# One audio tower layer on one Trainium2 core: new orders on all engines, mixing with 64 stationary columns, token weights through ScalarE's queue

## The chip, the cores and the metric

The kernel runs on one core of a Trainium2 chip. A core has TensorE (PE in the profile, its weight loads PEld), VectorE (DVE), ScalarE (ACT), GpSimd (POOL) and SyncE (SP). TensorE writes into PSUM, which has 8 banks of 512 fp32 values in each of 128 partitions; everything else lies in SBUF. The metric is the device time of one execution in microseconds (us), lower is better. The kernel before took 1020.71 us as the median of three runs (1018.73 to 1024.64).

## The reference, cut to what matters

```python
# x [128 batches, 64 features, 750 steps], padded to 752 = 94 windows of 8
scores  = einsum('bwkf,of->bwko', xp, w) + b          # token pooling
h       = sum(xp * softmax(scores, axis=2), axis=2)   # [128, 94, 64]
xn      = layernorm(h)
q, k    = xn @ Q[h], xn @ K[h]                        # 8 heads, rank 32
attn    = softmax(q @ k.T / sqrt(64))                 # [128, 8, 94, 94]
h       = h + sum_h (attn @ xn) @ VO[h]
h       = h + ffn(layernorm(h))
# ffn: 4 heads x 4 experts of causal attention with width 16, a gated sum of the
# experts, layernorm, two 16x16 layers with a mask, layernorm, and a gate over the heads
```

All arithmetic is fp32. "Mixing" in the title is `attn @ xn`.

## The kernel before, in words

The 128 batches go through in 32 quads of four. Partitions hold 4 batches x 32 tokens, and the free dimension holds the three token blocks j = 0, 1, 2. Nothing is scheduled by the hardware or a compiler: each engine has its own function `quad(g)` that lists its steps in an order written out by hand, and calls it for g = 0 to 42 or 43. A step works on quad g - d, where d is the step's distance: so one call holds steps of up to 13 different quads, and the distances make a software pipeline. Steps wait on semaphores (`wait_ge`). PSUM banks are given to steps by number, so a step also waits until the last reader of its bank is done.

The steps on TensorE, with their lines, in the order in which a quad meets them: `tok_score` (L598, token scores for two quads at a time), `tok_turn` (L612), `turn` (L588, transposes of x into three banks), `pool_x` (L606, the pooled h), `turn_x` (L650), `project` (L657), `score` (L665, one call for each block j), `mix` (L676), `give_outT` (L686), `give_out` (L697), `front_turn` (L703), `front_pair` (L710), `front_sv` (L716, L719), `score3_a` (L743) and `score3_b` (L759), the expert scores, `turn_p3` (L766), `mix3` (L776), `turn_c` (L785), `turn_rest` (L803), `layer1` (L807), `layer2` (L811), `turn_fo` (L790) and `head_logits` (L797).

What lies around the places that the change touches:

- `mix` (L676) multiplies, for each block `ub`, the weights `pT` by `xn`. A stationary operand is a 32x32 piece of `xn`; the loops over 2 parities, 2 column halves `c` and 4 batches use all 16 pieces of the array. The accumulation runs over the three `ub`. An fp32 matmul is two LDWEIGHTS and two MATMUL instructions here. `mix` waits for ScalarE's `front_kp` (L1101) to empty its banks.
- `exp_s` (L1074) is the softmax exponential on ScalarE, 8 ACTIVATEs per block j; `exp_s(0)` follows `front_kp` directly, and `layer2` on TensorE waits for it, because both use bank 6. `copy_cT` (L1079) empties the mixed result and follows `exp_s(0)` on ScalarE.
- `soft` (L1368, L1370) is VectorE's maximum and subtraction for the expert scores; `soft(2)` follows `score3_a` and frees the banks for `mix3`.
- GpSimd applies the softmax denominators (`norm_p`, L462), the two steps of the layer norms with a power (`norm_power` L495, `ln_power` L450, `power3` L467) and the gates. VectorE's `turn_p(0)` (L1349) waits for `norm_p(0)`.
- Before the loops GpSimd clears constants and then loads the token weights and bias by three DMAs of its own (L414 to L416). TensorE waits for these three and for the x of quad 0 before the first `tok_score`.
- SyncE loads x for quads 0 to 5 first, the attention weights (q, k, vo) between them, then some 60 small, strided loads of the feed-forward weights (L346), and only then enters its own loop of x loads and stores. `make_g` (L620, once) needs the attention weights, `split_w` (L1300, L1301, VectorE, once) and after it `make_w` (L629, TensorE, once) need all of the feed-forward weights.

On TensorE before, the calls begin as follows: g = 0 is `tok_score(0)`; g = 1 is `make_g`, `tok_turn`, two of the `turn`s of quad 0; g = 2 is the third `turn`, `pool_x(0)`, `tok_score(2)`, two `turn`s of quad 1; g = 3 is the third, `turn_x(0)`, `pool_x(1)`, `project(0)`, the three `score(0)`, `tok_turn`, `make_w`, two `turn`s of quad 2; g = 4 is the third, `turn_x(1)`, `pool_x(2)`, `project(1)`, `score(1)`, `mix(0)`, `score(1, j=2)`, `give_outT(0)`, `tok_score(4)`, `give_out(0)`, and two `turn`s of quad 3.

Of the kernel before, what the change touches and what calls it, by code (L numbers as in the profile page):

```python
# [15 lines left out]
TP = 96  # L16
# [26 lines left out]
def audio_tower(nc, x, tok_w, tok_b, attn_q, attn_k, attn_vo, hl_w, hl_b, wq, wk, wv, gate_w, gate_b,  # L43
                ln_g, ln_b, fc1_w, fc1_b, fc2_w, fc2_b, fnorm_g, fnorm_b, fgate_w, out):
    with ExitStack() as ctx:
# [24 lines left out]
        zeroed = sem("zeroed")  # L70
        zeroed2 = sem("zeroed2")
# [255 lines left out]
        def _(sp):  # L327
# [57 lines left out]
            def quad(g):  # L385
                if exists(g + 6, NQUAD):
                    sp.wait_ge(x_turned, 3 * g + 3)
                    load(g + 6)
                if exists(g - 12, TAIL):
                    sp.wait_ge(ho_made, 3 * g - 33)  # L390
                    store(g - 12, (g - 12) % 2)
                if TAIL <= g - 12 < NQUAD:
                    sp.wait_ge(ho_made_late, 3 * g - 120)
                    store(g - 12, (g - 12) % 2)

            for g in range(44):
                quad(g)
# [5 lines left out]
        def _(pool):  # L403
            pool.memset(ident_w[:, :], 0.0).then_inc(zeroed, 1)
# [4 lines left out]
            pool.memset(tw[:, :], 0.0).then_inc(zeroed, 1)  # L409
            pool.memset(wp[:, :, :, :], 0.0).then_inc(zeroed, 1)  # L410
            pool.memset(xs[:, :, NTIME:128 * NCH], 0.0).then_inc(zeroed, 1)
            pool.wait_ge(zeroed, 8)
# [111 lines left out]
            def quad(g):  # L524
                if exists(g - 11, TAIL):
                    finish(g - 11)
                if exists(g, NQUAD):
                    if g < 4:
                        pool.wait_ge(tok_ready, (g) // 2 + 1)
                    weigh(g)  # L530
# [3 lines left out]
                if exists(g - 2, NQUAD):  # L534
                    pool.wait_ge(at_summed, 3 * g - 3)
                    norm_p(1, at_normed)
                if exists(g - 2, NQUAD):
                    norm_p(2, at_normed)
                if exists(g - 6, NQUAD):
                    pool.wait_ge(y_eps, g - 5)  # L540
                    norm_power(g - 6, 0, y_rstd)
# [3 lines left out]
                if exists(g - 6, TAIL):  # L545
                    pool.wait_ge(y_rstd, 2 * g - 10)
                    scale(0, y_mul)
# [3 lines left out]
                if exists(g - 1, NQUAD):  # L551
                    pool.wait_ge(at_summed, 3 * g - 2)
                    norm_p(0, at_normed)
                if exists(g - 7, TAIL):
                    pool.wait_ge(t_made, g - 6)
                    residual()
                if exists(g - 8, NQUAD):
                    if g - 8 >= 28:
                        pool.wait_ge(z_eps, g - 7)
                    norm_power(g - 8, 1, z_rstd)  # L560
                if exists(g - 5, NQUAD):
                    pool.wait_ge(g_inv, 2 * g - 8)
                    gate_weight(g - 5)
                if exists(g - 6, TAIL):
                    norm_affine(g - 6, 0, fx_made, "j h", fx[:, :, 0:96].rearrange("p h (j c) -> p j h c", c=32))
                if exists(g - 5, NQUAD):
                    pool.wait_ge(g_weight, 2 * g - 8)
                    gate_mul((g - 5) % 2)
# [3 lines left out]
                if exists(g - 2, NQUAD):  # L572
                    pool.wait_ge(ln3_var, 2 * g - 2)
                    power3(g - 2)
                if exists(g - 8, TAIL):
                    scale(1, z_mul)
# [5 lines left out]
        def _(pe):  # L582
# [62 lines left out]
            pe.wait_ge(zeroed, 8)  # L645
# [168 lines left out]
            def quad(g):  # L814
                if exists(g - 7, NQUAD):
                    if g - 7 >= 29:
                        pe.wait_ge(t_made, g - 9)
                    if g - 7 < 29:
                        pe.wait_ge(at_exped, 3 * g - 9)
                    turn_p3(4, 6, p_turned)  # L820
                if exists(g - 7, NQUAD):
                    if g - 7 < 27:
                        pe.wait_ge(x_copied, 2 * g - 3)
                    if 27 <= g - 7 < 30:
                        pe.wait_ge(at_added, g - 4)
                    turn_p3(3, 0, p_turned)
                if exists(g - 12, NQUAD):
                    pe.wait_ge(fo_copied, g - 11)
                    head_logits(7)
                if exists(g - 2, NQUAD):  # L830
                    if g - 2 >= 5:
                        pe.wait_ge(p_exped, 6 * g - 37)
                    if 2 <= g - 2 < 5:
                        pe.wait_ge(at_exped, 3 * g - 9)
                    turn(g - 2, 2, 6, x_turned)
                if g - 1 == 0:
                    make_g(3)
                if g - 6 == 0:
                    front_resid(7)
                if exists(g - 9, NQUAD):  # L840
                    if g - 9 < 30:
                        pe.wait_ge(p_exped, 6 * g - 36)
                    if g - 9 >= 29:
                        pe.wait_ge(fx_made_late, 2 * g - 74)
                    if g - 9 < 29:
                        pe.wait_ge(fx_made, 2 * g - 16)
                    turn_rest(fx[:, :, :], 0, r1_fxt)
                if exists(g - 7, NQUAD):
                    if g - 7 < 27:
                        pe.wait_ge(x_copied, 2 * g - 2)  # L850
                    if g - 7 < 31:
                        pe.wait_ge(s_shifted2, 2 * g - 10)
                    mix3(g - 7, 1)
                if exists(g - 3, NQUAD):
                    if g - 3 < 4:
                        pe.wait_ge(x_copied, 2 * g - 3)
                    if g - 3 >= 6:
                        pe.wait_ge(r1_fxc, g - 8)
# [738 lines left out]
```

## Time and profile before

| | |
|---|---|
| median of three runs | 1020.71 us |
| profiled execution, device time | 1028.39 us |
| profiled execution, span of the trace | 1026.7 us |
| instructions | 53,493 |
| busy: PE, PEld | 875.7 us (85%), 602.5 us (59%) |
| busy: DVE, ACT, POOL | 754.3, 741.7, 693.8 us (73%, 72%, 68%) |
| chain that ended last | PE 62%, ACT 17%, DVE 11%, issue 4%, SPq 4%, POOL 2% |
| granted TensorE clock, mean | 0.963 |

The profiled execution is 7.7 us slower than the median of the runs. A share of the chain is the part of the span for which the work followed back from the end stood on that engine. "Issue" is time in which an engine waited for nothing that the profile shows. TensorE's busy time is the union of overlapping matmuls, whose ends are modelled.

### The profile page before, as it was taken

To read this page: it belongs to the slowest core of one execution; us is meant where nothing else is said; L and a number is where in the kernel's file an instruction comes from. 1 tells how busy PE (TensorE), PEld (TensorE's weight loads), DVE (VectorE), ACT (ScalarE), POOL (GpSimd) and SP (SyncE) were. 2 spreads that over 40 slices of the span, in tenths; PEclk is the share of its full clock that TensorE was granted. 3 is DMA by queue.
4 is the path that set the end of the run, shared out by engine and by line. 5 is a ranking of instruction groups with operands and counts; after the bars stand their busy time and mean duration, and the time that the engine had idled before them with its cause. 6 is when DMAs were issued, how large, how long until landed. Compare 5 with 4: busy or idle time off the path is not lost.

```text
span 1026.7 us, 53493 instructions
## 1 busy us (share of the span) xinstructions
PE 875.7 (85%) x23616; PEld 602.5 (59%) x23616; DVE 754.3 (73%) x1786; ACT 741.7 (72%) x2631; POOL 693.8 (68%) x1087
## 2 busy tenths in 40 slices
PE   4488988998898989899999999998998998887853
PEld 3365655665665656566676666665676665555531
DVE  2346677777777788778888788877888888776765
ACT  1567777887777888777887788887887787774521
POOL 3343345666678677677788777776777877766684
PEclk9789999999999999999999999999999999999965
DMA  6211111001111110011111111001000000000000
GB/s 191 66 62 33 33 34 33 27 11 33 33 33 37 38 36 24 18 38 37 38 38 38 37 37 38 15 27 41 7 9 7 7 7 7 4 8 6 11 8 21
DMA packets 34504, 31.47 MB, mean 31 GB/s; under 512 B 26080, under 2 KB 26080, under 8 KB 34272
## 3 DMA queue, kind: packets, MB, share of 16 engines
q1 hardware_dynamic: 33926, 28.00, 9.4%
q8 instruction: 185, 3.03, 1.2%
q14 instruction: 47, 0.39, 0.1%
q10 hardware_dynamic: 250, 0.05, 0.0%
q0 software_dynamic: 96, 0.00, 0.0%
HBM read 24.95 MB, written 3.08 MB: 27 GB/s over the span
## 4 chain that ended last, share of the span: by engine, by line
PE 62%; ACT 17%; DVE 11%; issue 4%; SPq 4%; POOL 2%; DMA 0%; POOLq 0%
PE psum L676 8%; ACT pu L1074 8%; PE psum L776 7%; PE psum L785 6%; PE psum L766 6%; PE psum L657 4%; PE psum L759 4%; PE psum L710 4%; DVE pu L1370 4%; DVE mx L1368 4%; ACT cT L1079 3%; PE psum L665 3%; SPq L346 2%; PE psum L606 2%; ACT kp L1101 2%
## 5 line engine op out<-in xcount | busy, mean ns | idle before, releaser
L1074 ACT ACTIVATE pu<-psum,mx 128x94 f32<-128x94 f32 x768 | 250.7, 386 | 4.0 <-DVE mx L1343 4.0
L1074 ACT ACTIVATION_READ_ACCUMULATOR pu<-psum,mx 128x1 f32 x768 | 194.7, 254 | 0.0
L462 POOL TENSOR_TENSOR pu<-pu,pr 128x752 f32<-128x752 f32 x96 | 137.4, 1445 | 23.9 <-DVE pr L1346 23.8
L1368 DVE TENSOR_REDUCE mx<-psum 128x16 f32<-128x1536 f32 (+2 forms) x96 | 117.2, 1221 | 48.3 <-PE psum L759 30.7
L495 POOL TENSOR_TENSOR st<-st,neg_half 128x12 f32<-128x12 f32 x64 | 146.2, 2285 | 5.0
L448 POOL TENSOR_TENSOR ln_ve<-ln_mv,eps_c 128x3 f32<-128x3 f32 x32 | 6.2, 193 | 178.8 <-DVE ln_mv L1338 178.8
L1343 DVE TENSOR_REDUCE mx<-psum 128x8 f32<-128x752 f32 x96 | 89.0, 927 | 46.1 <-PE psum L665 46.1
L1370 DVE TENSOR_TENSOR pu<-psum,mx 128x1536 f32<-128x1536 f32 (+2 forms) x96 | 117.6, 1225 | 3.3
L665 PE MATMUL psum<-kp,xT 64*32 64x376 f32 x1536 | 103.1, 486 | 17.4 <-DVE ft L1440 11.6
L1112 ACT ACTIVATE pT<-psum 128x512 f32<-128x512 f32 x192 | 104.5, 595 | 14.4 <-PE psum L766 12.5
L766 PE MATMUL psum<-ident_w,pu 128*128 128x128 f32 x768 | 102.1, 277 | 1.0 <-ACT pu L1074 0.6
L676 PE MATMUL psum<-pT,xn 32*32 32x384 f32 x3072 | 88.5, 491 | 9.6 <-ACT kp L1101 8.6
L1349 DVE STREAM_TRANSPOSE pT<-pu 128x768 f32<-128x768 f32 x96 | 89.7, 958 | 4.5 <-POOL pu L462 4.5
L766 PEld LDWEIGHTS psum<-ident_w,pu 128*128 128x128 f32 x768 | 87.6, 142 | 3.9 <-ACT pu L1074 1.2
L1375 DVE SCALAR_TENSOR_TENSOR ct<-sxT,psum 128x512 f32<-128x512 f32 x96 | 60.3, 684 | 32.3 <-PE psum L776 32.3
L785 PE MATMUL psum<-gx,ct 128*32 128x84 f32 x3072 | 74.1, 242 | 8.2 <-issue 6.7
L776 PE MATMUL psum<-pT,vv 32*32 32x384 f32 (+2 forms) x3072 | 70.9, 403 | 10.9 <-DVE pu L1370 9.7
L676 PEld LDWEIGHTS psum<-pT,xn 32*32 32x32 f32 x3072 | 45.2, 103 | 52.4 <-ACT kp L1101 30.7
L785 PEld LDWEIGHTS psum<-gx,ct 128*32 128x32 f32 x3072 | 61.9, 139 | 21.8 <-issue 19.5
L1115 ACT ACTIVATE oc<-psum 128x336 f32<-128x336 f32 x96 | 43.3, 452 | 38.8 <-PE psum L785 32.1
L1064 ACT ACTIVATE xT<-psum 128x384 f32<-128x384 f32 x32 | 15.7, 491 | 72.5 <-PE psum L650 72.4
L710 PE MATMUL psum<-x3T,aq 64*32 64x384 f32 x1024 | 65.8, 483 | 1.2 <-ACT hx L1121 1.2
(185 smaller groups left out, 2123.8 us busy)
## 6 DMA issues: line engine op xcount, KB each, us to landing
xs<-in_x SPq DMA_DIRECT2D x64, 375.0 KB, 3.8
out_h<-ho SPq DMA_DIRECT2D x126, 16.0 KB, 1.8
out_h<-ho SPq DMA_DIRECT2D x126, 7.5 KB, 1.8
gx<-in_L_ffn_gate_w SPq DMA_DIRECT2D x16, 0.2 KB
fc<-in_L_ffn_fc_w SPq DMA_DIRECT2D x12, 1.0 KB
fc<-in_L_ffn_fc_b SPq DMA_DIRECT2D x12, 0.1 KB
vo_w<-in_L_attn_VO SPq DMA_DIRECT2D x2, 64.0 KB, 8.7
q_w<-in_L_attn_Q SPq DMA_DIRECT2D x1, 64.0 KB, 7.8
```

Of the source, the lines that this page charges most:

```text
L462: pool.tensor_tensor(p, p, bcast(pr[:, j, :, :].rearrange("p a b -> p (a b)"), 2, NTOK), ALU.mult).then_inc(done, 1)
L495: pool.tensor_tensor(st[:, k, 3, :], st[:, k, 2, :], neg_half[:, 0:NJ * NH], ALU.pow).then_inc(rstd, 1)
L665: mm = pe.matmul(psum[TB * b:TB * b + TB, bank + par, 0:HP * NTOK], xT[rows, n % 2, b, TB * j:TB * j + TB], kp[rows, n % 2, b, :, 0:NTOK], ...
L676: mm = pe.matmul(psum[q:q + 32, bank + b, 0:HP * TP].rearrange("p (h j t) -> p h j t", h=HP, j=NT), xn[rows, n % 4, ub, 0, 32 * c:32 * c + ...
L710: mm = pe.matmul(psum[32 * n:32 * n + 32, bank + half, 0:NJ * 128], aq[rows, e + half, n, :], x3T[rows, :, :].rearrange("p b t -> p (b t)" ...
L766: mm = pe.transpose(psum[:, bank, 128 * e:128 * e + 128], pu3[j][:, e, k, :, :].rearrange("p b u -> p (b u)"), ident)
L776: mm = pe.matmul(psum[QB * n:QB * n + QB, bank + b, 128 * k:3 * 128].rearrange("p (j t e) -> p j e t", e=NE, t=QB), vv[rows, n3 % 2, k, n, ...
L785: mm = pe.matmul(psum[rows, bank, GC * e:GC * e + GC], ct3[:, j, rows, e], gx[:, e, :], start=True, stop=True)
L1074: ins = act.activation(pu[:, j, par, hp, 0:NTOK], psum[:, bank + par, NTOK * hp:NTOK * hp + NTOK], ACT.Exp, bias=mx[:, j, par, hp:hp + 1], ...
L1112: act.activation(pT3[:, SLOT3[P3[f]], :, :].rearrange("p e c -> p (e c)"), psum[:, bank, :], ACT.Exp).then_inc(done, 1)
L1368: dve.tensor_reduce(mx3[:, j, :, :], S3(j, bank), AX.X, ALU.max).then_inc(shifted, 1)
L1370: dve.tensor_tensor(pu3[j][:, :, :, :, :].rearrange("p e k b u -> p b e k u"), S3(j, bank).rearrange("p b e (k u) -> p b e k u", u=QB), bc ...
```

## The change

1. `mix`: the stationary operand is now 64 columns wide (`xn[rows, ..., :]`), so a matmul fills a 32x64 piece of the array; the loop over `c` is gone, and the order is `ub`, batch, parity. 24 matmuls for each quad in place of 48.
2. The token weights and the bias are loaded by ScalarE's queue, the bias without any wait, the weights after a semaphore of their own (`tw_zeroed`) that GpSimd's first instruction sets.
3. The order inside `quad(g)` is new on all four computing engines, with other distances, other waits and other PSUM banks. On TensorE the call now begins where `score(j=2)` stood: most of the new distances are the old ones less one, because the loop's start was moved by most of a call. Apart from that start, `turn_x` comes before `mix3`, `turn_rest` after it, `turn_p3(4)` between two `turn`s, `layer1` before `front_turn`.
4. `make_g` moves from g = 1 to g = 2, behind `turn(1)`; `make_w` from g = 3 to g = 4, behind `give_out(0)`.
5. SyncE stores quad g - 13 instead of g - 12 and runs 45 calls in place of 44; TensorE runs 43 calls in place of 44.

TensorE's first calls are now: g = 0 `tok_score(0)`; g = 1 `tok_turn`, the three `turn`s of quad 0, `pool_x(0)`; g = 2 `tok_score(2)`, three `turn`s, `make_g`, `turn_x(0)`, `pool_x(1)`, `project(0)`, `score(0)` for j = 0, 1; g = 3 `score(0, j=2)`, `tok_turn`, three `turn`s of quad 2, `turn_x(1)`, `pool_x(2)`, `project(1)`, `score(1)`, `mix(0)`; g = 4 `score(1, j=2)`, `give_outT(0)`, `tok_score(4)`, `give_out(0)`, `make_w`, `turn`s of quad 3.

```diff
@@ SyncE, quad(g)
-                if exists(g - 12, TAIL):
-                    sp.wait_ge(ho_made, 3 * g - 33)
-                    store(g - 12, (g - 12) % 2)
+                if exists(g - 13, TAIL):
+                    sp.wait_ge(ho_made, 3 * g - 36)
+                    store(g - 13, (g - 13) % 2)
@@ GpSimd, start
+            pool.memset(tw[:, :], 0.0).then_inc(tw_zeroed, 1)
             pool.memset(ident_w[:, :], 0.0).then_inc(zeroed, 1)
...
-            pool.dma_start(tw[0:NFEAT, 26:27], tok_w.rearrange("o f -> f o")).then_inc(tok_loaded, 16)
-            pool.dma_start(tw[NFEAT:128, 32:33], tok_w.rearrange("o f -> f o")).then_inc(tok_loaded, 16)
-            pool.dma_start(tokb[:, :], tok_b.partition_broadcast(128)).then_inc(tok_loaded, 16)
@@ GpSimd, quad(g): the new order, waits left out
+   norm_power(g-9, 1), residual (g-8), norm_p(0) (g-2), scale(0) (g-7), gate_weight(g-6), scale(1) (g-9),
+   gate_mul (g-6), norm_affine(g-7, 0), norm_affine(g-9, 1), norm_p(1) (g-2), weigh(g), power3(g-3),
+   norm_p(2) (g-2), finish(g-11), norm_power(g-6, 0), ln_power(g), gate_scale (g-5), ln_apply(g)
@@ GpSimd, quad(g): the order before
-   finish(g-11), weigh(g), norm_affine(g-9, 1), norm_p(1), norm_p(2) (g-2), norm_power(g-6, 0), ln_power(g),
-   scale(0) (g-6), gate_scale (g-5), norm_p(0) (g-1), residual (g-7), norm_power(g-8, 1), gate_weight(g-5),
-   norm_affine(g-6, 0), gate_mul (g-5), ln_apply(g), power3(g-2), scale(1) (g-8)
@@ TensorE, mix
                 for ub in range(NT):
-                    for par in range(2):
-                        for c in range(2):
-                            for b in range(4):
-                                rows = slice(TB * b, TB * b + TB)
-                                q = 64 * par + 32 * c
-                                mm = pe.matmul(psum[q:q + 32, bank + b, 0:HP * TP].rearrange("p (h j t) -> p h j t", h=HP, j=NT),
-                                               xn[rows, n % 4, ub, 0, 32 * c:32 * c + 32],
-                                               pT[rows, :, par, :, ub, :].rearrange("p j h t -> p h j t"), start=(ub == 0), stop=(ub == NT - 1))
+                    for b in range(4):
+                        rows = slice(TB * b, TB * b + TB)
+                        for par in range(2):
+                            mm = pe.matmul(psum[64 * par:64 * par + 64, bank + b, 0:HP * TP].rearrange("p (h j t) -> p h j t", h=HP, j=NT),
+                                           xn[rows, n % 4, ub, 0, :], pT[rows, :, par, :, ub, :].rearrange("p j h t -> p h j t"),
+                                           start=(ub == 0), stop=(ub == NT - 1))
@@ TensorE, quad(g), steady part: the new order, waits left out, banks in brackets
+   score j=2 (g-3) [6], give_outT(g-4) [2], tok_score(g) [0], tok_turn [3], give_out(g-4) [1], score3_a(g-5) [2],
+   turn 0 (g-1) [1], turn_p3 4 (g-6) [0], turn 1 (g-1) [6], turn_fo(g-11) [7], turn_p3 3 (g-6) [1], turn 2 (g-1) [0],
+   turn_x(g-2) [7], head_logits(g-11) [6], mix3(g-6) [1], turn_rest (g-8) [5], turn_p3 0, 1 (g-5) [6, 7],
+   turn_c 0 (g-6) [5], score3_b(g-5) [0], turn_c 2, 1 (g-6) [7, 5], pool_x(g-1) [4], turn_p3 2 (g-5) [6],
+   layer1 (g-8) [7], front_turn (g-4) [5], turn_p3 5 (g-5) [4], project(g-2) [6, 2], front_pair 0 (g-4) [4],
+   front_sv [0], score j=0 (g-2) [6], front_pair 2 [2], score j=1 [4], mix(g-3) [0], layer2 (g-8) [6]
@@ ScalarE, start
+            act.dma_start(tokb[:, :], tok_b.partition_broadcast(128)).then_inc(tok_loaded, 16)
+            act.wait_ge(tw_zeroed, 1)
+            act.dma_start(tw[0:NFEAT, 26:27], tok_w.rearrange("o f -> f o")).then_inc(tok_loaded, 16)
+            act.dma_start(tw[NFEAT:128, 32:33], tok_w.rearrange("o f -> f o")).then_inc(tok_loaded, 16)
@@ VectorE, quad(g), steady part: the new order, waits left out
+   head_sum(g-12), sums 0 (g-3), mask_second (g-9), least 2 (g-3), turn_p 0 (g-3), sums 1 (g-3), gate_sum(g-7),
+   soft_tok(g), add_out(g-4), soft(g-5, j=2), head_shift(g-11), stats3(g-4), copy_x 2 (g-1), sums 2 (g-3),
+   guard 0, 1, 2 (g-6), mix_experts(g-7), centre(g-9), soft j=0 (g-5), variance(0) (g-7), soft j=1, sums_inv (g-6),
+   ln_stats(g-1), turn_p 1, mask_hidden (g-8), turn_p 2, variance(1) (g-9), least 0 (g-2), gate_shift(g-6), least 1
...
```

## Rows read from the trace of the kernel before

**Rows 1.** Stretches of the span: length, then each engine's busy us (instructions), clock, DMA.
```profile
0.00:81.50 81.50, 50.23 (x923) 35.86 (x925) 28.66 (x102) 36.96 (x140) 28.78 (x62) 0.85 0.36 101
512.63:568.66 56.03, 52.28 (x1465) 36.51 (x1465) 45.84 (x110) 45.94 (x165) 43.72 (x68) 1.00 0.12 35
934.80:1026.70 91.90, 54.48 (x1247) 36.03 (x1247) 57.80 (x155) 28.75 (x74) 59.19 (x88) 0.75 0.05 11
```

**Rows 2.** Chain that ended last, two calls: start us, us, what.
```profile
511.77 0.82 ACT kp L1101
...
512.63 2.77 PE psum L676 x94
515.40 0.63 PE psum L811 x4
...
525.45 2.11 PE psum L776 x73
```

**Rows 3.** The same chain over the whole span, starts of mixing: first, clean pair, last.
```profile
133.94 2.78 PE psum L676 x94
...
540.25 2.78 PE psum L676 x94
...
880.92 2.78 PE psum L676 x94
```

**Rows 4.** A stretch inside mixing: busy PE (count), PEld (count), clock, DMA.
```profile
513.45:513.80 0.35, 0.35 (x33) 0.31 (x31) 1.00 0.20 47
```

**Rows 5.** TensorE's timeline, projection; then its group by shape (busy us, mean ns).
```profile
507.23 1.52 PE L657 MATMUL psum<-xT,g_w 64*32 64x384 f32 x32
...
L657 PE MATMUL psum<-xT,g_w 64*32 64x384 f32 x1024 | 50.1, 497 | 1.6 <-DVE pu L1370 0.9 <-ACT pT L1112 0.7
```

**Rows 6.** ScalarE's timeline around mixing.
```profile
514.68 0.38 ACT L1074 ACTIVATE pu<-psum,mx 128x94 f32<-128x94 f32 x1
515.43 1.51 ACT L1079 ACTIVATE cT<-psum 128x768 f32<-128x768 f32 x2 [0.28 <-PE psum L676]
```

**Rows 7.** Waits over the whole span: total us, times, longest us.
```profile
PEld psum L811 <- ACT pu L1074: 16.3, 26, 0.6
PEld psum L606 <- issue: 15.3, 14, 1.6
```

**Rows 8.** Timeline of the start, POOL's queue and TensorE.
```profile
4.35 0.57 POOL L416 DMA_DIRECT2D tokb<-in_L_tok_b  x1
...
11.96 2.79 PE L598 MATMUL psum<-xs,tw 128*32 128x128 f32 x48 [11.96 <-DMA tokb<-in_L_tok_b]
...
16.80 1.59 PE L620 MATMUL psum<-q_w,k_w 32*64 32x64 f32 x16 [2.05 <-DMA vo_w<-in_L_attn_VO]
16.81 0.29 DVE L1287 TENSOR_TENSOR tok_e<-tok_e,tok_r 128x128 f32<-128x128 f32 x1
18.32 0.47 PE L612 MATMUL psum<-ident_w,tok_e 128*128 128x128 f32 x1
```

**Rows 9.** Loads of x for quad 0 (issued 0.8 to 2.2): us to landing.
```profile
DMA to landing us min/median/max: 3.4/4.5/5.7
```

**Rows 10.** Timeline of TensorE from 39 us to 66 us.
```profile
39.02 0.48 PE L612 MATMUL psum<-ident_w,tok_e 128*128 128x128 f32 x1 [0.40 <-DVE tok_e L1287]
...
64.43 0.54 PE L697 MATMUL psum<-ident_w,oT 64*32 64x64 f32 x24
```

**Rows 11.** Chain of the start: the last feed-forward weight, then `make_w`.
```profile
41.12 4.85 DMA bet<-in_L_ffn_fnorm_b
...
46.94 1.03 PE psum L629 x32
```

**Rows 12.** DMA queue of TensorE's instructions: packets, MB, share of 16 engines.
```profile
q8 instruction: 185, 3.03, 1.2%
```

**Rows 13.** GpSimd and VectorE around the first softmax block.
```profile
515.50 1.44 POOL L462 TENSOR_TENSOR pu<-pu,pr 128x752 f32<-128x752 f32 x1
518.34 0.96 DVE L1349 STREAM_TRANSPOSE pT<-pu 128x768 f32<-128x768 f32 x1
```

More of the change, by code:

```diff
@@ L827, in quad @@
[L827 to L853, printed above, removed]
@@ L966, in quad @@
                     pe.wait_ge(at_cT, 2 * g - 6)
[L967 removed]
+                    give_outT(2)
+                if exists(g, NQUAD) and (g) % 2 == 0:
+                    tok_score(g, 0)
                 if exists(g - 1, NQUAD) and (g - 1) % 2 == 0:
[L969 to L972 removed]
+                    if g - 1 < 7:
+                        pe.wait_ge(tok_normed, (g - 1) // 2 + 1)
+                    tok_turn(3)
                 if exists(g - 4, NQUAD):
                     pe.wait_ge(at_oT, g - 3)
[L975 to L976 removed]
+                    give_out(1)
+                if g - 4 == 0:
                     pe.wait_ge(w_split, 1)
[L978 removed]
+                    make_w(2)
                 if exists(g - 5, NQUAD):
@@ new lines, in quad @@
+                if exists(g - 1, NQUAD):
+                    if g - 1 >= 5:
+                        pe.wait_ge(p_exped, 6 * g - 31)
+                    if g - 1 == 1:
+                        pe.wait_ge(tok_shifted, (g + 1) // 2 + 1)
+                    if g - 1 == 3:
+                        pe.wait_ge(tok_shifted, (g + 1) // 2 + 1)
+                    turn(g - 1, 2, 0, x_turned)
+                if exists(g - 2, NQUAD):
+                    if g - 2 >= 9:
+                        pe.wait_ge(fo_copied, g - 10)
+                    if g - 2 < 2:
+                        pe.wait_ge(ln_done, 2 * g - 2)
+                    turn_x(g - 2, 7)
@@ L1027, in _ @@
+                if exists(g - 8, NQUAD):
+                    if g - 8 < 26:
+                        pe.wait_ge(at_exped, 3 * g - 5)
+                    pe.wait_ge(h_masked, g - 7)
+                    layer2(6)
+            for g in range(0, 43):
                 quad(g)
@@ L1136, in quad @@
             def quad(g):
+                if exists(g - 4, NQUAD):
+                    act.wait_ge(at_mixed, g - 3)
+                    copy_cT(1, 0, at_cT)
+                if exists(g - 4, NQUAD):
+                    copy_cT(0, 0, at_cT)
+                if exists(g - 3, NQUAD):
+                    act.wait_ge(at_maxed, 3 * g - 7)
+                    exp_s(1, 4, at_exped)
+                if exists(g - 4, NQUAD):
+                    act.wait_ge(at_outT, g - 3)
+                    copy_oT(2)
@@ new lines, in quad @@
+                if exists(g - 1, NQUAD) and (g - 1) % 2 == 0:
+                    act.wait_ge(tok_turned, (g - 1) // 2 + 1)
+                    copy_tok(g - 1, 3)
+                if exists(g - 7, NQUAD):
+                    if g - 7 >= 28:
+                        act.wait_ge(g_shifted, 3 * g - 18)
+                    gate_exp()
+                if exists(g - 3, NQUAD):
+                    act.wait_ge(at_maxed, 3 * g - 6)
+                    exp_s(2, 6, at_exped)
+                if g - 4 == 0:
+                    act.wait_ge(w_made, 1)
+                    copy_m(2)
@@ new lines, in quad @@
+                if exists(g - 5, NQUAD):
+                    soft(g - 5, 1, 0, s_shifted1)
+                if exists(g - 6, NQUAD):
+                    dve.wait_ge(c_copied, 3 * g - 15)
+                    sums_inv((g - 6) % 2)
+                if exists(g - 1, NQUAD):
+                    dve.wait_ge(h_pooled, g)
+                    ln_stats(g - 1)
+                if exists(g - 3, NQUAD):
+                    turn_p(1, at_pturned)
+                if exists(g - 8, NQUAD):
+                    dve.wait_ge(r1_hx, g - 7)
+                    mask_hidden()
```

667 lines of the change are left out of this document (323 added, 344 removed).

## The prediction

> **What bounds the kernel now.** I read the stretches first, then the chain that ended last, the waits on it, and the timelines around single steps. The span has three parts. The fill (0 to 81.5 us) has TensorE busy for only 50.2 us, the steady part 52.3 of every 56.0, and the tail from 934.8 us 54.5 of 91.9 [rows 1]. In the steady part TensorE is the bound at the full clock: its mixing is on the chain in every call, and starts 747.0 us apart from the first to the last of 26 calls, 28.73 us a call [rows 3]. The pair 512.63 to 540.25 takes 27.6 us [rows 2, 3], so an average call loses 1.1 us that a clean one doesn't. Most of it is "issue" idleness in the dense runs of small matmuls: 14 waits before L606 alone, up to 1.6 us each, 15.3 us in all [rows 7].
>
> **Change 1, mixing.** 96 MATMULs take 2.77 us on the chain [rows 2]. They go through the array as 3 rounds (`ub`) of 2 passes. What a pass costs where loads keep up is shown by the projection: 4 passes of 8 pieces with the same 384 columns take 1.52 us [rows 5]; less one matmul's 0.50 us at the end [rows 5] that is 3 steps of 0.34. Six passes at that price are 5 x 0.34 + 0.50 = 2.2 us. Mixing takes 0.57 us longer, and a row shows how: within its second round 31 weight loads are issued in 0.35 us [rows 4], so they had not been pulled ahead of the matmuls, as a round of 16 pieces is 64 instructions. The new rounds have 8 pieces and 32 instructions, like the projection's. I take 2.2 us: a gain of 0.57 us for each quad. Bounds: 0, if what costs is the columns and not the loads; and a loss, if 32x64 pieces with four row groups don't run side by side. No row has such a piece, so the worst end is by the projection's passes at double number: 12 steps, 11 x 0.34 + 0.5 = 4.2 us, a loss of 1.5 us for each quad.
> The Trainium skill (TensorE: Matmul & The Clock Gate, Part 2: What happens when you issue a matmul) gives TensorE a window of 64 instructions in which it pulls weight loads ahead. The row agrees with that reading; the sum doesn't need it.
>
> How much of 0.57 us reaches the end? `front_kp` on ScalarE (0.82 us from 511.77) releases mixing and then starts `exp_s(0)` at once [rows 2]. Its last ACTIVATE starts at 514.68 and, with its accumulator read, is over at about 515.15 [rows 6]; `layer2`, next on TensorE, waits for exactly that in 26 calls [rows 7]. Mixing ends at 515.40 [rows 2]. So in the calls where TensorE is the chain, `layer2` gains about 0.15 us, not 0.57. Where ScalarE is the chain (the other parity, in which `give_out` waits for it), `copy_cT` had been idle 0.28 us for mixing [rows 6] and gains that. 16 x 0.15 + 16 x 0.28 = 7 us; **I take -6**, ends 0 and -18 (0.57 x 32, if nothing hides it).
>
> **Change 3, the orders.** Listed by quad and not by call, nearly every distance is unchanged: the call starts elsewhere. What remains on TensorE is a swap around `mix3` (`turn_x` before, `turn_rest` behind) and new banks. In one parity `mix3` waits for VectorE's `soft(2)` (it starts at 525.45 [rows 2], after `score3_a` plus two passes of VectorE), in the other for copies on ScalarE whose sum is the same; neither list is shorter. I cost it at 0. Cover: the 0.05 us that the swap adds before `mix3` lies in that wait. On GpSimd `norm_p(0)` now stands behind `norm_power(1)` and `residual`, which waits for VectorE's `mask_second`. Before, it ran 515.50 to 516.9 and `turn_p(0)` took its result only at 518.34 [rows 13]. I place it about 1.5 us later, which ends at 518.4, just when VectorE arrives, and VectorE then waits anyway for `exp_s(1)`. GpSimd is busy 43.7 of 56.0 us [rows 1], so it can hold the order. Bounds: nothing to 2 us a call, see the fourth rival. The tail has the same steps at the same distances: 0, with 4 us either way.
>
> **Change 2 and 4, the start.** (a) TensorE starts at 11.96, held by the bias, which GpSimd issued at 4.35 as the third of its loads [rows 8]. x of quad 0 needs at most 5.7 us after an issue at 2.2 at the latest, so it is there at 7.9 [rows 9]. ScalarE's queue has nothing before and can issue near 0.8 to 2.5 us. If its landing takes the bias's 7.4 us (4.35 to 11.75), TensorE starts at 9 to 10, if as long as x, at 8. Gain 2 to 4, I take 3.5. The Trainium skill (DMA: Bandwidth & Descriptors, SWDGE vs HWDGE vs iDMA) says that the queue of ScalarE makes descriptors in hardware and sets up faster than GpSimd's; by that it would be the 4. (b) `make_g` waits for the attention weights and holds `tok_turn`, which starts at 18.32 though its input is ready at 17.1 [rows 8]: -1.2. It comes back later at its own 1.6 us [rows 8]: +1.6. (c) After `tok_turn` at 39.02 to 39.5 TensorE has nothing but `make_w`, which waits for the last feed-forward weight (landing at 46.0) and starts at 46.94 [rows 10, 11]. The new order puts the steps from `turn(2)` to `give_out(0)` before it, which now run from 47.97 to 64.97, 17.0 us [rows 10, 11]. New: 39.5 - 3.1 + 17.0 = 53.4, past 46.9, so `make_w` no longer waits, and the 7.4 us of idleness are filled. Sum: 3.5 + 1.2 - 1.6 + 7.4 = 10.5 us; **I take -11** with the better chance of a warm clock. Bounds: -5 (the freed time is eaten by the latency of softmax chains, that before ran during the wait) to -15.
>
> **Instruction supply.** TensorE's instructions come in 185 packets of 3.03 MB [rows 12], 256 instructions of 64 bytes each, and the losses before L606 are at every 256th. A boundary costs only if it falls in the dense run from `turn_c` to `pool_x`. Counting positions through both lists (47,232 instructions before, 3,072 fewer now), 17 calls were hit before and about 13 would be now, at about 1.8 us. **I take -5**, for the count slips easily; ends +5 and -15.
>
> **Change 5.** A later store is cost at 0: the buffers' next writer is 2 quads away, and at the end the last store still follows the last result.
>
> **Sum.** -6 - 11 - 5 = -22 us. Against the profiled execution's 1028.4 that is 1006.4; it stood 7.7 above the median of the runs, and for the median I subtract the same 22 us: 1020.7 - 22 = **999 us**.
>
> **The rivals.**
> 1. *Mixing is bound by columns and the supply doesn't improve.* Only the start remains: -11, 1010 us. For it: a pass of 384 columns costs the same in both shapes; against: rows 4. The Trainium skill (TensorEngine Tiling (Array Packing), Overview) measures the gain by the number of pieces: 3 rounds before, 3 rounds now, nothing gained. Its time is this one; the trace bears it out only in part, since 16 pieces cost more a pass than 8. Chance 0.22.
> 2. *The cover of mixing is thinner than I read*, so 0.57 us goes through in most calls, and supply gains 10: -11 - 16 - 10 = -37, 984 us. Against: `layer2`'s wait [rows 7]. Chance 0.15.
> 3. *Slower: the 32x64 pieces don't run side by side.* Mixing becomes 4.2 us, past `exp_s(0)`, so all of +1.45 reaches the end in each of 32 quads: +46 - 11 - 5, 1051 us. It decides as soon as mixing lasts over 2.9 us. Against: `score` and projection run 8 pieces in two row groups. Chance 0.05.
> 4. *GpSimd's order is late.* If `norm_p(0)` ends over 1 us after 518.4, `turn_p(0)` holds VectorE, `soft(2)` and `mix3` behind it, at about 0.7 us a call: +22 - 22 = 0, 1021 us. Against: GpSimd's idleness of 6 us a call. Chance 0.08.
>
> **How the numbers follow.** My forecast has 0.50. The 8 in 10 range takes rival 1, most of 2 and the bounds of the start: 982 to 1015. The likeliest case alone spans 992 to 1006. A measurement here tells 0.5% (5 us) from no change: faster than 1015.6 is my case, rivals 1 and 2 nearly whole, 0.85; within 5 us 0.07; slower 0.08 (rival 3 and the bad half of 4).
>
> **What would show it.** In the new profile: mixing at 2.2 us on the chain, but the next `layer2` waiting for `exp_s(0)` for longer than 0.6 us; the first `tok_score` at 8 to 10 us; `make_w` without a wait at about 53 us; `mix3` preceded by the same waits; fewer "issue" losses at L606, L759, L785; a clean call near 27.4. I am wrong if mixing doesn't shrink, if `turn_p(0)` waits for GpSimd in most calls, or if the early scores come no sooner than before.

## The result, and the profile after

The changed kernel takes 996.7 us (median of 4 runs, 996.1 to 1000.1), the kernel before, beside it on the same chip, 1021.6 us (4 runs, 1018.7 to 1024.6). The ratio is 0.9757, with a 95% interval of 0.9722 to 0.9792: 25 us less, where the forecast said 22. The profiled executions are further apart, 1028.4 against 996.1 us, and so are their spans, 1026.7 and 994.4 us: the one of before stood above its median, the one of after at it.

The stretches of the span, cut as in [rows 1] at the second start of mixing, over two calls, and from the last start of mixing (length, then each engine's busy us and instructions, clock, DMA):

```profile
0.00:70.70 70.70, 46.49 (x870) 32.84 (x870) 29.55 (x103) 36.93 (x140) 30.03 (x64) 0.86 0.38 116
487.99:545.10 57.11, 51.33 (x1369) 35.76 (x1369) 46.22 (x109) 45.75 (x166) 45.06 (x69) 1.00 0.11 34
906.10:994.40 88.30, 50.88 (x1199) 34.72 (x1199) 57.10 (x152) 28.00 (x74) 58.71 (x87) 0.79 0.05 12
```

The fill is 10.8 us shorter than in [rows 1] and the tail 3.6. The two calls are 1.1 us longer than the pair of [rows 1]; each call of this pair has a halt of the instruction stream, and the first of that one had none. A pair says little here; 26 calls say more, below.

The groups of mixing and projection by shape (busy us, mean ns), and then the queue of TensorE's instructions (packets, MB), which answer to [rows 2, 5] and [rows 12]:

```profile
L675 PE MATMUL psum<-pT,xn 32*64 32x384 f32 x1536 | 70.2, 490 | 9.5 <-ACT kp L1110 9.5
...
L658 PE MATMUL psum<-xT,g_w 64*32 64x384 f32 x1024 | 50.1, 494 | 0.1
```
```profile
q8 instruction: 173, 2.83, 1.1%
```

Mixing keeps TensorE busy for 70.2 / 32 = 2.19 us a quad: the forecast's 2.2. A stretch of the second round, as [rows 4] (busy PE, PEld, DVE, ACT, POOL, clock, DMA):

```profile
488.90:489.25 0.35, 0.35 (x23) 0.21 (x12) 0.35 (x2) 0.35 (x4) 0.35 (x1) 1.00 0.00 0
```

12 weight loads issue in 0.35 us, where it was 31. Half of that drop is the halved number of loads. The rest is their pace: in the trace groups of 8 matmuls now follow each other by 0.34 us, nearly all with 8 loads, while before a round's 31 or 32 loads fell into 0.35 us and the round's last matmuls went on without any. The Trainium skill (TensorE: Matmul & The Clock Gate, Part 2: What happens when you issue a matmul) has loads pulled ahead within 64 instructions; with rounds of 32 instructions this row agrees. No run changed the number of instructions in a round alone, so that the window is what cost the 0.57 us is not shown.

The chain that ended last, around one start of mixing, and the wait of `layer2` on `exp_s(0)` over the whole span, which answer to [rows 2, 7]:

```profile
487.18 0.81 ACT kp L1110
487.99 2.58 ACT pu L1083 x16
490.57 0.04 issue
490.61 0.70 PE psum L810 x4
491.31 0.02 issue
491.33 0.37 DVE ft L1451
```
```profile
PEld psum L810 <- ACT pu L1083: 27.1, 26, 1.0
```

Mixing has left the chain. The step from the copy of kp goes through ScalarE's exponentials (L1083) to `layer2` (L810); that wait grew from 16.3 to 27.1 us over 26 calls, from 0.63 to 1.04 us a call. So 0.41 of the 0.57 us turn into waiting there: it is the cover that the prediction named.

GpSimd and VectorE around the first softmax block, which answer to [rows 13]:

```profile
492.32 1.45 POOL L460 TENSOR_TENSOR pu<-pu,pr 128x752 f32<-128x752 f32 x1
493.80 0.98 DVE L1360 STREAM_TRANSPOSE pT<-pu 128x768 f32<-128x768 f32 x1
```

Counted from the start of mixing, `norm_p(0)` runs 4.33 us later, where it ran 2.87 later before: moved by 1.5 us as worked out. VectorE takes its result 5.81 us after that start, against 5.71 before. Its own work lasts until then, and in none of the 96 times does it wait for GpSimd (4 times before, 4.5 us): nothing is lost.

The chain of the start:

```profile
2.19 6.37 DMA xs<-in_x
8.57 0.14 issue
8.70 2.79 PE psum L599 x48
...
13.87 0.33 PE psum L613
...
53.45 0.03 DVE whl L1311
53.48 0.32 DVE whl L1312
53.80 1.33 DVE whl L1311
55.12 0.32 DVE whl L1312
...
57.04 1.53 PE psum L589 x12
```

The first scoring of tokens (L599) now waits for x itself and starts at 8.70, not 11.96; `tok_turn` starts at 13.87, not 18.32. `make_w` is held by VectorE's `split_w` (L1311, L1312) rather than by a DMA. The first full `turn` behind it starts at 57.04; it was at 65.79.

Last, what the prediction called instruction supply. A stretch of the chain in the dense part of a call, in the changed kernel's first profile, and the same call in a second profile of the same kernel (e12):

```profile
506.33 1.33 PE psum L784 x64
507.66 0.44 PE psum L607 x31
508.10 0.57 issue
508.67 0.44 PE psum L607 x17
509.11 0.59 PE psum L765 x4
```
```profile
504.67 1.33 PE psum L784 x64
506.00 0.44 PE psum L607 x31
506.44 1.12 issue
507.56 0.44 PE psum L607 x17
508.00 0.59 PE psum L765 x4
```

In both, `pool_x` stops behind the same matmul, its 31st, with nothing to wait for: once for 0.57 us, once for 1.12. I call this a halt, and count it from the traces' list of TensorE's instructions: an instruction that starts over 0.15 us after the one before it, and whose place in the list is 193 plus a multiple of 256. (A true wait that falls there is counted too.) In the kernel before the halts of the 26 calls come to 30.7 us, in the changed one to 20.6. By the waits over the whole span the idleness without a releaser fell too: of the weight loads from 15.3 to 10.1 us at `pool_x` [rows 7], from 6.7 to 3.0 at `score3_b` and from 19.5 to 16.0 at `turn_c`, but it rose from 9.1 to 16.0 at `mix3`. The prediction had the waits before `mix3` unchanged, and they aren't: its MATMULs wait for VectorE's `soft` for 21.4 us in 31 calls, before for 9.7 us in 18.

### The profile page after: what moved, and what is told of

Its sections match the earlier page's. It is cut to its first block, busy times and chain, and to the rows that moved or that the text cites. A ratio compares the mean times of both kernels' runs of the same rounds, so it can differ in the third digit from the quotient of the medians.

```text
span 994.4 us, 50395 instructions
## 1 busy us (share of the span) xinstructions
PE 847.6 (85%) x22080; PEld 588.5 (59%) x22080; DVE 756.6 (76%) x1786; ACT 737.6 (74%) x2631; POOL 694.4 (70%) x1084
## 4 chain that ended last, share of the span: by engine, by line
PE 57%; ACT 21%; DVE 16%; issue 3%; POOL 2%; DMA 1%; POOLq 0%; SPq 0%; DVEq 0%
ACT pu L1083 13%; PE psum L775 7%; DVE pu L1381 6%; DVE mx L1379 6%; PE psum L784 6%; PE psum L765 6%; PE psum L658 5%; PE psum L709 4%; PE psum L758 4%; PE psum L742 3%; PE psum L666 3%; ACT cT L1088 3%; PE psum L607 3%; ACT kp L1110 3%; PE psum L599 2%
## 5 line engine op out<-in xcount | busy, mean ns | idle before, releaser
L1083 ACT ACTIVATE pu<-psum,mx 128x94 f32<-128x94 f32 x768 | 254.4, 425 | 4.0 <-DVE mx L1354 4.0
L1083 ACT ACTIVATION_READ_ACCUMULATOR pu<-psum,mx 128x1 f32 x768 | 215.5, 293 | 0.0
L1121 ACT ACTIVATE pT<-psum 128x512 f32<-128x512 f32 x192 | 115.1, 616 | 20.6 <-PE psum L765 19.9
L666 PE MATMUL psum<-kp,xT 64*32 64x376 f32 x1536 | 105.6, 485 | 19.4 <-DVE ft L1451 11.6
L765 PE MATMUL psum<-ident_w,pu 128*128 128x128 f32 x768 | 115.0, 280 | 1.5 <-DVE pu L1381 1.3
L775 PE MATMUL psum<-pT,vv 32*32 32x384 f32 (+2 forms) x3072 | 69.7, 396 | 21.6 <-DVE pu L1381 21.4
L1127 ACT ACTIVATE fxT<-psum 128x256 f32<-128x256 f32 x32 | 12.3, 384 | 95.0 <-PE psum L802 95.0
L675 PE MATMUL psum<-pT,xn 32*64 32x384 f32 x1536 | 70.2, 490 | 9.5 <-ACT kp L1110 9.5
L775 PEld LDWEIGHTS psum<-pT,vv 32*32 32x32 f32 x3072 | 45.0, 104 | 41.1 <-ACT pT L1121 16.2
L589 PE MATMUL psum<-ident_w,xs 128*128 128x128 f32 x384 | 61.6, 288 | 8.3 <-ACT pu L1083 6.8
L510 POOL TENSOR_TENSOR ft<-ft,fx 128x192 f32<-128x192 f32 x29 | 17.2, 594 | 68.7 <-DVE ft L1451 68.7
```

The source lines that it names most:

```text
L666: mm = pe.matmul(psum[TB * b:TB * b + TB, bank + par, 0:HP * NTOK], xT[rows, n % 2, b, TB * j:TB * j + TB], kp[rows, n % 2, b, :, 0:NTOK], ...
L765: mm = pe.transpose(psum[:, bank, 128 * e:128 * e + 128], pu3[j][:, e, k, :, :].rearrange("p b u -> p (b u)"), ident)
L775: mm = pe.matmul(psum[QB * n:QB * n + QB, bank + b, 128 * k:3 * 128].rearrange("p (j t e) -> p j e t", e=NE, t=QB), vv[rows, n3 % 2, k, n, ...
L1083: ins = act.activation(pu[:, j, par, hp, 0:NTOK], psum[:, bank + par, NTOK * hp:NTOK * hp + NTOK], ACT.Exp, bias=mx[:, j, par, hp:hp + 1], ...
L1121: act.activation(pT3[:, SLOT3[P3[f]], :, :].rearrange("p e c -> p (e c)"), psum[:, bank, :], ACT.Exp).then_inc(done, 1)
```

## The experiments

Eleven other kernels ran, and the changed one again (e12), each beside the kernel before (medians there 1022 to 1024 us). Ratios are to that kernel.

**e1 to e4: one part alone, or all but one.** The edit of e1 (e2 is its reverse, in the changed kernel):

```diff
-for par in range(2): for c in range(2): for b in range(4):
-    pe.matmul(psum[q:q + 32, ...], xn[rows, n % 4, ub, 0, 32 * c:32 * c + 32], pT[...])
+for b in range(4): for par in range(2):
+    pe.matmul(psum[64 * par:64 * par + 64, ...], xn[rows, n % 4, ub, 0, :], pT[...])
```

> The kernel before with the 64-column mixing alone. Theory A (the prediction's): a call's mixing falls from 2.77 to about 2.2 us, but the softmax's exponentials on ScalarE (2.58 us after the copy of kp) take its place as the end of that stretch, so only about 0.2 us of a call's 0.57 reach the end: some 6 us less than the kernel before, ratio about 0.994. Rival B: the whole 0.57 us of 32 calls reaches the end: 18 us less, ratio 0.982. Rival C: mixing was never on the path that sets the end: within 2 us. The change also takes 64 TensorE instructions out of each call, so it moves the places at which TensorE's stream halts without a wait; by a table from the trace before, their sum stays at 27 us, so no more than 3 us either way is expected of that.

> The changed kernel with the old 32-column mixing put back, all else as changed. Theory A: some 6 us more than the changed kernel (996.7), about 1003. Rival B (the whole 0.57 us of 32 calls): about 1015. Rival C: about 997. Theory S (the halts of TensorE's stream at every 256th instruction depend on which instruction stands there): the added instructions move the halts of the dense stretches, whose sum by a table from the two traces rises from 20 to some 30 us, so about 1010 with theory A.

Measured: e1 0.9948 (0.9923 to 0.9973), 5 us less. (It takes 96 instructions out of a call, not the 64 expected: 24 matmuls at 4.) e2 0.9943 (0.9913 to 0.9972), 1017.0 us: 20 us more than the changed kernel. So mixing seemed to be worth 5 us in one place and 20 in the other. Shares of the chain by line, e1 and then e2:

```profile
ACT pu L1072 16%; PE psum L774 7%; PE psum L783 7%; PE psum L764 5%; PE psum L657 4%; PE psum L708 4%; PE psum L757 4%; DVE pu L1368 4%; DVE mx L1366 4%; PE psum L665 3%; ACT cT L1077 3%; ACT kp L1099 3%; SPq L346 3%; PE psum L606 2%; PE psum L684 2%
```
```profile
PE psum L677 9%; PE psum L777 7%; PE psum L786 7%; PE psum L767 6%; DVE pu L1383 6%; DVE mx L1381 6%; ACT pu L1085 5%; PE psum L658 5%; PE psum L711 4%; PE psum L760 4%; PE psum L666 3%; ACT cT L1090 3%; PE psum L744 3%; PE psum L607 3%; ACT kp L1112 3%
```

In e1 mixing (L674) is gone from the list and the exponentials (L1072) have 16%, twice the 8% of L1074 before; in e2 mixing (L677) leads with 9%. The wait of `layer2` for the exponentials goes with mixing alone: 26.9 us in e1, 16.3 in e2, as 27.1 and 16.3 in the kernels of after and before. So the cover is shown both ways:

```profile
PEld psum L809 <- ACT pu L1072: 26.9, 26, 1.0
```
```profile
PEld psum L812 <- ACT pu L1085: 16.3, 26, 0.6
```

e2's time is that of rival B (1015) and not theory A's 1003; why it is not rival B's mechanism the table below tells.

The edits of the start, e3 the loads alone, e4 both:

```diff
-pool.dma_start(tokb[:, :], ...)          # and the two loads of tw
+act.dma_start(tokb[:, :], ...)           # first on ScalarE's queue
...
-if g - 3 == 0: make_w(3); copy_m(3)
+if g - 4 == 0: make_w(3); copy_m(3)      # and split_w later in that call
```

> The kernel before with the three token loads on ScalarE's queue alone. Theory A: the first scoring of tokens (L598) starts when x has landed, about 8.7 us, and not at 11.96, and the gain is carried to the end: 3.3 us less, about 1018. Rival D: the start is bound again further on, by the filter and the weights (make_w), so nothing reaches the end: within 1 us of the kernel before.

> The kernel before with both edits of the start: the token loads on ScalarE's queue, and the making of the second filter's weights (make_w, with the split and the copy that follow it) one call later. Theory A: the 7.4 us that TensorE waited for make_w are filled and 3.3 us come from the loads: 9 to 11 us less, about 1011. Rival D: the first front stages are bound elsewhere (VectorE's softmax of the tokens and split), so under 4 us: about 1018.

Measured: e3 1.0007 (0.9980 to 1.0034), no gain; e4 0.9893 (0.9866 to 0.9920), 10.9 us less. TensorE's timeline in e3:

```profile
9.67 2.79 PE L596 MATMUL psum<-xs,tw 128*32 128x128 f32 x48 [9.67 <-DMA xs<-in_x]
15.12 1.60 PE L618 MATMUL psum<-q_w,k_w 32*64 32x64 f32 x16 [2.66 <-DMA vo_w<-in_L_attn_VO]
16.65 0.47 PE L610 MATMUL psum<-ident_w,tok_e 128*128 128x128 f32 x1
```

The scoring starts 2.3 us sooner, but `make_g` (L618) still waits for the attention weights, which land at 15, and holds `tok_turn` (L610) to 16.65, 1.7 us sooner than in [rows 8]. Later the wait for `make_w` takes the rest: mixing of quad 0 starts at 56.7, before at 57.0.

**e5 and e8: do the parts add?** e5 is e1 and e4 in one; e8 is e4 with the loads left on GpSimd's queue.

> The kernel before with the 64-column mixing and both edits of the start. Singly these gave 5.1 us (mixing, e1) and 10.8 us (start, e4). Theory A (the terms add, and the new orders give nothing of their own): about 1007, and then the 10 us between this and the changed kernel (996.7) are neither mixing nor start, so the orders or the places of TensorE's halts. Rival M (mixing is worth more where the start is short): about 997, and the orders are worth nothing.

> The kernel before with the making of the second filter's weights one call later and the token loads left on GpSimd's queue. Theory A (the prediction's: the two edits are worth 7.4 and 3.5 us): 3 us more than the kernel with both edits (e4, 10.8 us under before), so about 7.5 us under before. Rival D: the loads are worth nothing with or without it (alone they gave nothing, e3): the same 10.8 us under before.

Measured: e5 0.9841 (0.9810 to 0.9872), 16.3 us less; e1 and e4 add up to 5.3 + 10.9 = 16.2. e8 0.9909 (0.9881 to 0.9937), 9.3 us less. Singly the parts add, and 8 us are left between e5 and the changed kernel (0.9764 in e12). e8 and e4 are 1.6 us apart, within their intervals; that the loads then count is not shown by it.

**Where each kernel's time is.** From the traces, in us: start of mixing of quad 3 (the fill), the 26 calls from there to that of quad 29, the halts within them, the mean of those calls with under 0.25 us of them, and from there to the end. The calls were also fitted, for each kernel by itself, to a straight line over their halts:

```
kernel                     fill   26 calls  halts  clean call  rest   us of call per us of halt
before                     133.9   747.0    30.7    27.48     145.7   1.03
e1 mixing                  134.5   730.9    22.6    27.26     144.3   1.03
e3 loads                   133.7   742.2    27.1    27.47     149.2   1.00
e8 make_w later            128.0   742.3    28.3    27.48     146.5   1.02
e4 e3 and e8               126.8   736.4    22.6    27.49     145.6   0.93
e5 e1 and e4               124.0   737.0    29.8    27.27     144.8   1.07
e2 after, mixing as before 130.4   743.3    30.7    none      148.8   1.04
after                      125.8   727.0    20.6    27.15     141.5   1.04
e12 after again            124.1   726.4    20.4    27.09     142.8   1.09
```

A microsecond of halt makes its call a microsecond longer, in every kernel. That is a fit over 26 calls, not an intervention, but nine kernels agree. And a clean call takes 27.47 to 27.49 us with the old mixing and old orders, 27.26 or 27.27 with the new mixing in them, and 27.09 to 27.15 in the changed kernel. With no halt at all the last two are 27.21 or 27.26 and 27.15 or 27.22, from 5 to 7 calls each: what the new orders give a clean call is not clear of that.

The list of TensorE's instructions doesn't fix the sum of the halts. From quad 2 on, the kernel before, e3, e4 and e8 have the same list, to within one instruction, and their halts are 30.7, 27.1, 22.6 and 28.3 us. The profiled executions of the four lie +5.4, +3.1, -1.7 and +3.6 us from their kernels' medians: about as much as their halts differ. So an execution's halts are part of its noise, and the halts of two single profiles compare kernels only roughly.

From before to after the spans differ by 32.3 us: fill 8.1, halts 30.7 - 20.6 = 10.1, the rest of the calls (747.0 - 30.7) - (727.0 - 20.6) = 9.9, tail 4.2. e2 against after, 28 us in the spans: fill 4.6, halts 10.1, rest of the calls 6.2, tail 7.3. So e2's 20 us in the medians are not mixing's own time: putting it back also adds 96 instructions a call, and so moves every later halt. How much of the 20 the halts are is not shown, as e2's profiled execution is 7 us slower than its median.

**e6, e7, e9, e10, e11: moving the halts.** In the traces up to then, a call had no halt between mix3 and pool_x if the first such place lay about 124 to 178 instructions behind the start of mix3. These kernels add instructions that compute nothing new, to bring it there or away from it.

```diff
+def pad(k):                                  # e6, e7: waits already met
+    for _ in range(k): pe.wait_ge(tw_zeroed, 1)
...
+for i in range(fills.get(n, 0)):             # e9, e10, e11: ahead of mix
+    pe.matmul(psum[64 * par:64 * par + 32, bank + b, 0:1], xn[..., 0:32], pT[..., 0:1], start=True, stop=True)
```

> The changed kernel with waits that are already met put into TensorE's stream: 112 ahead of its first instruction, and 62 spread over four places in every second call (654 in all), so that the first 256th instruction after the start of each call's layer-2 mixing (mix3) falls on its 124th to 182nd instruction in 20 of the 26 calls from the fifth on. Theory S: in all traces so far the stretch from mix3 to pool_x takes 7.4 to 7.5 us and has no halt where that instruction lies between 124 and 205, and 8.2 to 10 us elsewhere; most of the changed kernel's 20.6 us of halts go, less what the added waits cost (650 of 20 to 50 ns, most while TensorE waits anyway): 8 to 17 us less, 980 to 989. Rival W: the halts come from something in time (a transfer, another engine), not from the place in the stream: no gain, and up to 10 us more for the waits, 997 to 1007.

> The same 654 met waits at the same places, with 72 more between the first scoring of tokens and the first transposition, where TensorE waits about 2 us anyway: all later instructions are the same as in the run before it, 72 places further on, so that the 256th instruction falls on the 61st or the 110th of mix3. Theory S: a halt of about 1.2 us in nearly every call, so about 30 us over the run against about 5 us of the kernel with 72 fewer: 20 to 30 us slower than that one, 1005 to 1015. Rival W: the same time as that one within 2 us.

> The changed kernel with tiny matmuls (32 columns of weights, one moving column, into PSUM cells that mix writes over) ahead of mix: 56 instructions before mix(0) and mix(1) each, and 62 before every second later mix, so that by the trace of the changed kernel the 256th instruction of TensorE's stream falls on the 127th or the 176th instruction from the start of mix3 in the calls of n = 4 to 25. Theory S: those 22 calls have no halt between mix3 and pool_x (0 to 0.3 us each, the run of 7.4 us), where the changed kernel had 17 us; less about 0.4 us for each of 10 groups: 10 to 15 us under the changed kernel in the same session. Rival W (the halts follow time or transfers): the same halts at other calls, no gain.

> The same with 96 more of the tiny instructions before mix(0) and mix(1), all later ones the same: the 256th instruction falls on the 31st or the 80th of mix3. Theory S: about 1.4 us in each of the 22 calls, 30 us of halts, and 20 to 30 us more than the kernel with 96 fewer. Rival W: within 2 us of it.

> The kernel before with the 64-column mixing and both edits of the start (e5, whose profile has 29.5 us of halts), and tiny matmuls ahead of mix, placed so that the 256th instruction falls on the 148th or the 199th from the start of mix3. Theory S: nearly all of the 25 us of halts of those calls go, 15 to 22 us less than e5, 986 to 994, and the new orders by themselves are worth what then separates it from the changed kernel placed in the same way. Rival W: no gain on e5, 1008.

> The changed kernel again, beside the three others on the same chip: 996 to 1001, with halts of 18 to 24 us at the same calls as in its first profile if they hang on the place in the stream alone (theory S), at other calls if not.

Measured, with the halts of the 26 calls counted as in the table: e6 0.9802 (1005.2 us) with 25.4 us, e7 0.9826 (1006.9) with 24.8; e9 0.9888 (1010.2) with 26.5, e10 0.9880 (1009.2) with 25.8; e11 0.9871 (1008.4) with 22.4, e5 having 29.8; e12 0.9764 (0.9731 to 0.9798) with 20.4, the first profile 20.6. Not one gained. The reason is in the traces: the placings were not the ones planned. Two of the added waits make one instruction in most places (654 waits gave 374), and one of the tiny f32 matmuls makes four (369 gave 1,476 instructions), not the two that I had counted. So "good" and "bad" both passed through all places in turn, their halts are alike, and their times with them. As a test of what a good placing is worth, these five failed, and it stays untried.

They do show three things. First, e12 halts at the same calls as the first profile; per call, the two correlate with 0.91. The kernel before and e3 do with 0.94, but e4 and e8 only with 0.65, though both have one list: two calls have 1.8 and 2.2 us of halts in e8 and none in e4. Second, where instructions were put in, the halts moved as the place says. With the new orders (after and e2, e6, e7, e9, e10, e12; the 24 calls from quad 2 on each) by the distance of the first place from mix3:

```
distance   124-177  178-212  213-240  241-255  0-60   61-123
calls         34       18       23       14     37      42
mean halt   0.02     0.40     0.63     1.66    1.46    1.28  us
```

None of the 34 calls in the first column has a halt over 0.25 us; 77 of the 79 in the last two have. With the old orders the free stretch is 124 to 212, 51 of 53 calls. Rival W in its plain form, that halts follow time and not the place, falls. Third, an added wait costs, and not only by itself. In e6 `layer2` (L821) starts 0.24 us after the exponentials, and 0.04 in the changed kernel. The added waits there, 106 ns each and not the 20 to 50 expected, were over 0.6 us earlier; but `layer2`'s own two waits now stand in the trace as instructions of their own.

```profile
496.79 2.57 ACT pu L1098 x16
499.36 0.24 issue
499.60 0.67 PE psum L821 x4
```

**What a halt waits for.** The traces also list the packets of the queue that moves TensorE's instructions, and there are as many as places at every 256th instruction. They are paired here in order, the first packet with the second place, in all 14 traces between 130 and 880 us. The packet of a place starts 0.85 us (median) after the place before it was passed and takes 0.99 us. The instruction at the place never starts sooner than 1.17 us after the end of its packet, and 387 of the 424 halts end 1.17 to 1.60 us after it; where there is no halt, the median is 3.4 us. Where TensorE went through the 256 instructions ahead of a place in under 3.0 us, halt left out, 250 of 268 places halted; over 4.0 us, 89 of 1466, true waits among them. So the halt ends when the next instructions have arrived, and it appears where TensorE uses them up faster than they come. Here rival W is half right: a transfer ends the halt, but the place in the stream sets when the transfer starts and how soon its instructions are needed. This is read from traces; no run changed the transfers.

## Why the prediction came out right

Its sum was -22, measured is -25 (medians); the terms, in the profiles that it was worked out from:

- *Mixing 2.77 to 2.2 us, of which -6 reach the end.* The duration is 2.19. Alone it gives -5.3 us (-7.9 to -2.8, moved halts among it), and 0.22 us a clean call. The cover was read rightly: `exp_s(0)` ends what mixing ended before. Rival 1 (columns bind, nothing gained) falls with e1; so does the forecast's reading of the Trainium skill (TensorEngine Tiling (Array Packing), Overview), which gives speedups by the number of pieces as upper bounds ("Up to 16×"): 3 rounds of 16 pieces and 3 of 8 would cost the same, and they take 2.77 and 2.19 us. Rival 3 (pieces not side by side) falls with 2.19 against its 4.2 us.
- *The start -11.* Both edits give -10.9 in the medians (e4, 8.2 to 13.7), and 11.0 between e1 and e5. The fills of single profiles, halts among them, are shorter by 7.1 (e4), 10.5 (e1 to e5), 8.1 (after) and 9.8 us (e12). The term was of the right size, but one of its parts was wrong: the loads' -3.5 is not there by itself (e3), because `make_g` and then `make_w` set the same times. In the changed kernel ScalarE issues the loads at 0.8 to 1.8 us, where GpSimd did at 3.1 to 4.35, and x is the last to land; the gain ended there. The Trainium skill (DMA: Bandwidth & Descriptors, SWDGE vs HWDGE vs iDMA) has the setup of ScalarE's queue faster than GpSimd's: here the bias took 4.7 us from issue to landing and not 7.4, but the weights 5.7 (median) on either queue, so it is the earlier issue that counts. The later `make_w` was worth 6.0 us of fill by itself (e8) against 7.4 predicted, and brought the first mixing from 57.0 to 49.3 us. The forecast had it without a wait at 53: its wait went from the DMA to `split_w`, 1.5 us on TensorE.
- *Instruction supply -5.* This step had the wrong mechanism, and whether its size was right can't be told. It had fewer hits at the same price, 13 for 17 at 1.8 us. Measured are 17 calls with over 0.25 us of halts before, as counted, but 18 and 19 after (e12); a hit costs 1.1 us in place of 1.8. Why it costs less is open. The profiled pair gives -10.1 us; against the mean of the four profiles with the old list (27.2) the changed kernel's 20.6 and 20.4 give -6.7.
- *Orders and tail 0.* Between e5 and the changed kernel are 8 us. In the profiles it is 11.5 us of span: halts 9.2, the rest of the calls 0.8, the tail 3.3, and the fill 1.8 the other way. By this pair what the orders gave is mostly halts; but e1, with e5's instructions from quad 2 on, has 22.6 us of them against e5's 29.8, so the 9.2 may as well be 2. The orders' own worth stays open; the tail, cost at nothing, gained 2 to 3 us with them (e5 against both profiles of after).
- *Rival 2, the cover is thinner, 984.* Of 0.57 us a call, mixing brings 0.22 in the clean calls of e1, and 6.2 / 26 = 0.24 a call between e2 and after. *Rival 4, GpSimd late:* `norm_p(0)` comes 1.5 us later, as worked out, and VectorE doesn't wait.

The total is partly luck. Mixing and start were read rightly; the -5 for the halts came from a count of hits that didn't fall, and the tail's 2 to 3 us were not foreseen. In the profiled pair, 32.3 us apart, the sum of 22 would have been 10 short; the profiled execution of before stood 5 to 8 us above the medians, and I had subtracted from the median. Halts at the same place differ between executions (0.57 and 1.12 us above), and the four profiles with the old list say that they are most of what that execution had more of.

## What to carry to other kernels

Before giving a shortened step its whole gain, name the engine that finishes next and how long after; here ScalarE's exponentials ended about 0.2 us before the mixing, and so kept 0.35 of 0.57 us a call. In a kernel bound by TensorE with short matmuls, sum the idleness that has no releaser by its place in the instruction stream: an edit that adds or removes instructions moves it, and can change the time by more than its own work does, so compare two versions by calls without such a halt. Profile the same list more than once before reading a difference of halts as the change's: here one list had 22.6 to 30.7 us. And before placing instructions by number, look in a trace how many the call really makes.

## What the runs showed of the hardware

- TensorE can halt at every 256th instruction, for up to 2.1 us at one place and 3.7 us in one call (both in the kernel before), when it went through the 256 ahead in under about 3 us. The instruction queue moves 185 packets before and 173 after for 3,072 fewer instructions, 256 for each packet.
- A packet starts 0.85 us after the place before is passed and takes 0.99 us (medians), and the instruction at its place starts at the soonest 1.17 us after its end (2,044 places in 14 traces).
- Whether it halts depends on where the place lies in the dense stretch: 0.02 us on average at 124 to 177 instructions from its start, 1.3 to 1.7 us from 241 round to 123 (seven traces with the new orders).
- A met wait that is an instruction of its own took TensorE 106 ns to the next such one (e6, median of 284 pairs). 654 added waits made 374 such instructions.
- Mixing with 64 stationary columns and 384 moving ones, 8 pieces a round, takes 2.19 us; with 32 columns and 16 pieces a round 2.77 us, for the same number of passes over the columns.
